# A Macaron layer with relative attention: the order of TensorE's work within an attention step

## What is computed

```
x = x + 0.5 * tanh(layernorm(x) @ W @ A1 @ A2 + b)
x = x + attention(layernorm(x))
x = x + 0.5 * tanh(layernorm(x) @ W @ A1 @ A2 + b)
```

```
content = (q + u) @ k.T                 # 1024 x 1024
pos     = relative_shift((q + v) @ p.T) # 1024 x 1024, row i is shifted by i
head    = softmax((content + pos) / 4) @ v
```

## Time and profile before

| | |
|---|---|
| median of three runs | 3433.29 us (3432.21 to 3438.11) |
| the profiled execution | 3432.96 us |
| its span in the trace | 3431.2 us |
| PE busy | 3357.4 us (98%) |
| PE weight loads | 2081.5 us (61%) |
| DVE busy | 1941.3 us (57%) |
| ACT busy | 2329.2 us (68%) |
| POOL busy | 1326.9 us (39%) |
| DMA | 1231.27 MB, mean 359 GB/s |
| granted TensorE clock | 0.988 on average |

### The profile page before, as it was taken

The page is one execution under the profiler, slowest core; times in us unless marked ns, Lnnn a source line. Parts: engine busy times, 40 slices in busy tenths (PEclk is TensorE's granted clock), DMA queues, the critical chain, the costliest instruction groups (busy, mean ns, idle before and its releaser), DMA issues. The chain is left out here.

```text
span 3431.2 us, 110393 instructions
## 1 busy us (share of the span) xinstructions
PE 3357.4 (98%) x34876; PEld 2081.5 (61%) x34876; DVE 1941.3 (57%) x5651; ACT 2329.2 (68%) x3255; POOL 1326.9 (39%) x1341
## 2 busy tenths in 40 slices
PE   8996999999999999999999999999999999999988
PEld 5662566666666666666666666666666666666677
DVE  7771555555555555555555555555555555555557
ACT  3342777777777777777777777777777777777633
POOL 2110444444444444444444444444444444444400
PEclk9996999999999999999999999999999999999999
DMA  5977999999999999999999999999999999999862
GB/s 165 293 246 242 379 390 388 389 390 387 387 387 392 387 388 388 390 388 388 388 389 390 387 387 390 389 387 389 389 389 388 387 388 391 388 388 388 303 197 98
DMA packets 433554, 1231.27 MB, mean 359 GB/s; under 512 B 48993, under 2 KB 133473, under 8 KB 433505
## 3 DMA queue, kind: packets, MB, share of 16 engines
q1 hardware_dynamic: 430000, 1229.12, 95.6%
q10 hardware_dynamic: 3504, 1.53, 0.2%
HBM read 617.04 MB, written 613.43 MB: 359 GB/s over the span
## 5 line engine op out<-in xcount | busy, mean ns | idle before, releaser
L867 POOL TENSOR_SCALAR at_pos_in<-at_pos_in,at_neg_max 128x1024 f32<-128x1024 f32 x1024 | 1145.8, 1119 | 1660.4 <-DVE at_neg_max L830 1660.4
L792 ACT ACTIVATE at_pos_out<-at_ps_pos 128x1024 f32<-128x1024 f32 x1024 | 1049.2, 1025 | 530.8 <-PE at_ps_pos L704 530.8
L830 DVE CUSTOM_DVE_ANT_0 at_pos_in<-at_ps_con,at_pos_in 128x512 f32<-128x512 f32 x1024 | 708.3, 692 | 1188.8 <-PE at_ps_con L704 818.5
L704 PE MATMUL at_ps_con<-at_right,at_left 32*128 32x512 f32 x4096 | 1329.5, 641 | 0.0
L801 ACT ACTIVATE at_prob<-at_ps_turn 128x512 f32<-128x512 f32 x2048 | 1111.5, 595 | 283.1 <-PE at_ps_turn L737 241.8
L704 PE MATMUL at_ps_pos<-at_right,at_left 32*128 32x512 f32 x4096 | 1167.4, 646 | 33.6 <-DMA at_left<-scratch_queries 20.6
L737 PE MATMUL at_ps_turn<-keep_ident,at_pos_in 128*128 128x128 f32 x8192 | 1105.9, 278 | 0.0
L737 PEld LDWEIGHTS at_ps_turn<-keep_ident,at_pos_in 128*128 128x128 f32 x8192 | 890.6, 141 | 156.5 <-issue 154.9
L750 PEld LDWEIGHTS at_ps_pv<-at_prob,at_v_aug 128*32 128x32 f32 x16384 | 385.0, 109 | 773.6 <-issue 773.5
L830 DVE CUSTOM_DVE_ANT_0 at_pos_in<-at_ps_con,at_pos_in,at_neg_half 128x512 f32<-128x512 f32 x1024 | 768.7, 751 | 140.5 <-PE at_ps_con L704 6.1
L750 PE MATMUL at_ps_pv<-at_prob,at_v_aug 128*32 128x128 f32 x16384 | 659.3, 279 | 0.8 <-issue 0.8
(11 more groups left out here) (92 smaller groups left out, 1387.6 us busy)
## 6 DMA issues: line engine op xcount, KB each, us to landing
scratch_scores<-at_pos_out SPq DMA_DIRECT2D x1024, 512.0 KB, 7.3
at_pos_in<-scratch_scores SPq DMA_DIRECT2D x1024, 512.0 KB, 7.5
scratch_queries<-fr_qk SPq DMA_DIRECT2D x128, 256.0 KB, 3.9
at_left<-scratch_queries SPq DMA_DIRECT2D x127, 256.0 KB, 7.3
fr_x<-in_L_attn_x_dram SPq DMA_DIRECT2D x16, 512.0 KB, 7.1
scratch_x<-fr_x_bo SPq DMA_DIRECT2D x16, 512.0 KB, 4.9
scratch_keys<-fr_qk SPq DMA_DIRECT2D x32, 256.0 KB, 5.2
scratch_values<-fr_values SPq DMA_DIRECT2D x8, 1024.0 KB, 5.8
```

The source lines that it names most:

```text
L704: return pe.matmul(banks[:, n, :], left[side][rows, t.i * P:(t.i + 1) * P], right[side][rows, :], start=True, stop=True)
L792: act.activation(pos_out[:, t.slot, :], ps_pos[:, :, :].rearrange("p a m -> p (a m)"), ACT.Copy)\
L830: dve.tensor_tensor_reduce(pos_in[:, t.slot, keys], ps_con[:, n, :], pos_in[:, t.slot, keys], -SCALE, 3.0e38 if n == 0 else neg_half[:, t. ...
L867: pool.tensor_scalar(pos_in[:, t.slot, :], pos_in[:, t.slot, :], -1.0, neg_max[:, t.slot:t.slot + 1], ALU.mult, ALU.add).then_inc(shifted, 1)
```

## The change

`turn` moves up within PE's step, ahead of the value products and the heads' transpose. No instruction, wait, buffer or semaphore is added or taken away, and the other engines' lists stay as they are.

```diff
@@ -769,13 +769,13 @@
                     positional(Tile(r, t + LEAD), 1 - Tile(r, t + LEAD).side)
                 if Tile(r, t).real():
                     content(Tile(r, t), 1)
+                if Tile(r, t - 2).real():
+                    turn(Tile(r, t - 2))
                 part = (t - 6) % QUAD
                 if Tile(r, t - 6 - part).real():
                     times_values(Tile(r, t - 6 - part), part)
                 if part == 0 and Tile(r, t - 10).real():
                     turn_heads(Tile(r, t - 10))
-                if Tile(r, t - 2).real():
-                    turn(Tile(r, t - 2))
```

## The result

The changed kernel takes 3471.16 us, the median of four runs (3470.1 to 3471.55), against 3433.32 before: a ratio of 1.0107, 95% interval 1.009 to 1.0125. It is slower by 38 us; 3470 was forecast. The profiled execution took 3471.55 us.

What follows compares the result with a forecast made beforehand. PE, in a loop with DVE, was taken as the pace, with DMA full but not late. 3433 plus 38 for 254 lone heads, minus 0.6 at the end, gave 3470 us, range 3444 to 3484.

Steps and rivals of the forecast that it cites:

- Plain steps: PE steps without a head's transpose: three changes of shape before and after, products to strips taken as 0.57, cost 0.
- the doubled price (3546): Bound at products to strips: the change costs twice its present price, +0.15 per step, 3546 us; 3%.
- The head: Head's transpose in each fourth step, alone between two other shapes: 0.26 instead of 0.11, 254 x 0.15 = 38 us.
- The cycle of 11.55: Four PE steps, one with a head: 4 x 2.648 + 0.26 + 0.70 of waits = 11.55 us, from 11.40.
- The cover: Later products and head signals to DVE stay hidden: normalising ends 0.54 after S, DVE's next need 1.36, 0.8 us left.
- S: A PE step's first strip load; DVE starts its total 1.36 us after it.
- Rival (d): Products or head signal so late that DVE's total starts 0.1 late in half of the steps: 3496 us; 5%.
- C: First load of a step's second content strip on PE; waits for DVE, following 3.00 us after the previous S.
- Rivals (a) to (c): (a) strips slip under products, 3395, 8%; (b) order makes no difference, 3433, 4%; (c) lone head pays half, 3452, 5%.
- DMA is full but not late: DMA at 388 GB/s, share 1.02; reads of scores land in 7.5 us, issued 14 us ahead, so PE is the pace.
- the halving rule: In PE's loop with DVE, a PE stage longer by x in every step costs x/2 per step.
- y: Fall in the 1.36 us from S to DVE's start when its waits are reordered; expected gain y/2 per step.

Runs made afterwards that it cites:

- split turning: Kernel before with products (and head) placed between the two halves of the turning: 3509.26 us, 1.02 against the kernel before in its session.
- shorter reads: Three quarters of each read-back: order of before 3435.3 us, the same with DVE asking for the content strip last 3395.83, changed order 3472.14.
- the head alone in the order of before: Kernel before with only the head's transpose moved, between strips and products: 3471.28 us, 1.0091 against the kernel before in its session.
- head-beside-turning kernel: Changed kernel with the head's transpose moved back next to turning (strips, turning, head, products): 3435.94 us, 0.998 against the kernel before in its session.

## Why the prediction was right

**The pace.** PE with DVE's loop sets the step, half and half: confirmed from both sides, by +76 for 0.15 more on PE in each step and -39 for 0.086 less on DVE.

**Plain steps cost nothing.** Confirmed, with the one transition that no row of before had: products to strips takes 0.57, as assumed, so the doubled price (3546) did not come. Strips to turning is 1.05 and turning to products 1.02 in the loop: what was read off the first and last steps holds there.

**The head.** 0.26 in place of 0.11, paid in full: 254 x 0.15 = 38 us, and the loop grew by 38.2. The spans differ by 38.6 (3469.8 - 3431.2): the loop starts 1.0 later (first strip load at 308.43, was 307.41), and what follows its last strips is 0.6 shorter, as forecast. The medians differ by 37.8. That they agree this closely with the forecast owes something to the session: in the later ones the kernel before had medians of 3442 and 3444. The cycle of 11.55 came out to the hundredth. The only row that showed this price whole stood in the tail of the trace: in the loop of before no head stands between two other shapes.

**The cover.** Copy and normalising run under cover as worked out, 0.10 later than forecast (done 0.64 after S, not 0.54), with 0.7 us to spare. Rival (d) did not happen. One small cost that no step named: once in 16 steps, where the written loop of 16 steps (BODY) turns over, strips follow products by 0.69 and not 0.57,

```profile
2003.29 0.38 PEld L750 LDWEIGHTS at_ps_pv<-at_prob,at_v_aug 128*32 128x32 f32 x16 [0.17 <-issue]
2003.98 0.29 PEld L704 LDWEIGHTS at_ps_con<-at_right,at_left 32*128 32x128 f32 x2 [0.31 <-issue]
...
2004.20 0.18 PEld L704 LDWEIGHTS at_ps_con<-at_right,at_left 32*128 32x128 f32 x1
```

and the next wait at C is shorter by as much: it is 0.22 there (2003.98 to 2004.20) and 0.34 in the corresponding step of a later four (2015.42 to 2015.76), so nothing is lost. That this is the time in which PE's sequencer takes the branch is a guess; it was not tested.

**Rivals (a) to (c)** fall by the rows: the gap at products-to-strips is there (0.20), the lone head pays a whole change, not half, and the change costs 37 us with less DMA traffic too. Of the two rules weighed, the runs side with the Trainium skill's TensorEngine Tiling (Array Packing), Key Properties, by which a change of tiling mode drains TensorE. The traces show no drain as such, but a gap of the weight loader at every change of shape (0.11 us behind the lone head, 0.17 to 0.76 elsewhere), and 0.15 us for the lone head's change and for the split turning's. The other rule, of the Trainium skill's TensorE: Matmul & The Clock Gate, Step-by-step: what each phase is for, by which the next matmul's fill hides a drain, fits only the neighbours of one shape here: nine transposes take 0.11 each.

**What was too smooth** is the sentence that DMA is full but not late. It was true of the trace before, and so harmless for a change that slows the loop. But the room was small, and an expectation built on it missed by more than 80 us (3389 by the halving rule at the 0.086 that y turned out to be, 3472 measured).

## What to carry to other kernels

Count the changes of TensorE's tile shape along its program order before reordering: an instruction is cheap beside one of its shape (0.11 us here) and pays a whole change on top when it stands alone (0.26), and moving a group can strand its neighbour. Where two engines hand a single buffer back and forth, write the recurrence: here time saved or added on either counted half when it came in every step, and in full in a step that overshot. The rare steps at the start and the end of a loop show transitions that the loop itself never makes; read them before calling a cost unknown.

## What the hardware showed beyond that

The share of busy DMA tells nothing of its room. It is 1.02 at 388 GB/s with reads landing in 7.5 us, 1.02 at 382 GB/s with 12.3 us and a stalled loop, and still 0.99 at 342 GB/s with 4.8 us. The time to landing tells more: it is 4.8 us with the shorter reads and 6 to 12 with whole ones, though it is no gauge of the rate either (6.3 us at 384 GB/s in the changed kernel, 9.8 at 383 with the head alone in the order of before). The step of before, 2.85 us, seems to lie near the edge: at the same pace the trace of the head-beside-turning kernel has landings of 11.6 us, and repeated runs of the kernel before spread from 3432 to 3469 us, while the changed kernel, 1% slower in its loop, stays within 1.5 us in its four runs and the kernels with shorter reads within 4. That suggests that the spread is DMA's, and does not show it: the head-beside-turning kernel, at the same pace and with the later landings, stays within 6 us in ten runs, and none of the longer executions of the kernel before was profiled. Asking for some 1% more than the kernel before gave less in the one trace of it: 382 GB/s for 388.

Two semaphore waits that had been met, placed between the wait that mattered and the instruction, cost DVE 0.09 us per tile: with them ahead of it, the start behind S went from 1.36 to 1.27 us, in the changed order and with shorter reads alike.
